# The inverse square root in a serial layer-norm recurrence: from ScalarE's table to VectorE arithmetic

## What is computed

```python
def step(carry, x):
    W1_s, b1_s = carry
    xq, xk, xv, eta_mb = x
    Z1 = xk @ W1_s + b1_s
    grad = _ln_fused_l2_bwd(Z1, xv - xk, ln_w, ln_b)
    Attn1 = jnp.tril(xq @ xk.swapaxes(-1, -2))
    b1_bar = b1_s - jnp.tril(eta_mb) @ grad
    Z1_bar = xq @ W1_s - eta_mb * Attn1 @ grad + b1_bar
    last_eta = eta_mb[:, :, -1, :, None]
    W1_new = W1_s - (last_eta * xk).swapaxes(-1, -2) @ grad
    b1_new = b1_s - jnp.sum(last_eta * grad, axis=-2, keepdims=True)
    out = xq + _ln(Z1_bar, ln_w, ln_b)
    return ((W1_new, b1_new), out)
```

## Time and profile before

| | us |
|---|---|
| Median of 3 runs (274.95 to 276.9) | 275.07 |
| The profiled execution | 269.17 |
| its span (first to last instruction) | 267.4 |
| busy in it: PE / DVE / ACT / POOL | 224.5 / 208.6 / 137.7 / 116.0 |
| mean granted clock of TensorE | 0.877 |

### The profile page before, as it was taken

How to read it: one execution, slowest core, us unless ns; L and a number is a source line. 1 busy time by engine, 2 the same in 40 slices (tenths; PEclk the granted TensorE clock), 3 DMA queues, 4 the chain that set the end, 5 groups by cost and what they waited for, 6 DMA issues and landing times.

```text
span 267.4 us, 5174 instructions
## 1 busy us (share of the span) xinstructions
PE 224.5 (84%) x1812; PEld 165.0 (62%) x1812; DVE 208.6 (78%) x548; ACT 137.7 (51%) x297; POOL 116.0 (43%) x151
## 2 busy tenths in 40 slices
PE   8389949799588997899399966996999889993993
PEld 6276425548356776577277654775778668782862
DVE  0873599998996999599949993959695996978551
ACT  1040363807374574558047607580477466867581
POOL 1840656309856454272237311725452263416044
PEclk9955999568879999799979957799799979998599
DMA  6945200012001200300020012000200034000012
GB/s 214 420 137 192 64 1 2 0 17 70 0 2 16 74 0 2 85 2 0 7 79 0 2 18 67 2 0 7 79 4 0 7 79 157 2 4 0 0 73 86
DMA packets 21544, 13.21 MB, mean 49 GB/s; under 512 B 10512, under 2 KB 19728, under 8 KB 21008
## 3 DMA queue, kind: packets, MB, share of 16 engines
q1 hardware_dynamic: 21088, 11.84, 15.0%
q10 hardware_dynamic: 432, 1.06, 1.1%
HBM read 11.02 MB, written 1.84 MB: 48 GB/s over the span
## 4 chain that ended last, share of the span: by engine, by line
PE 42%; DVE 31%; ACT 14%; issue 6%; DMA 3%; POOL 2%; DVEq 0%; POOLq 0%; SPq 0%; ACTq 0%
PE bank L964 11%; PE bank L983 6%; PE bank L900 6%; DVE pr L764 4%; DVE dW L769 4%; PE bank L935 4%; DMA x_bt<-in_x_bt 3%; DVE bank L716 3%; DVE pr L705 3%; ACT L473 2%; PE bank L997 2%; PE bank L908 2%; PE bank L917 2%; PE bank L973 2%; PE bank L1011 2%
## 5 line engine op out<-in xcount | busy, mean ns | idle before, releaser
L313 POOL TENSOR_TENSOR hh<-gate,upw 128x256 f32<-128x256 f32 x32 | 24.7, 772 | 56.8 <-ACT upw L460 56.8
L266 POOL TENSOR_TENSOR A<-A,mask 128x256 f32<-128x256 f32 x32 | 23.4, 733 | 38.4 <-ACT A L443 38.4
L935 PE MATMUL bank<-xqm,xkT 32*32 32x128 f32 x512 | 22.2, 291 | 20.5 <-DVE QP L654 11.5
L983 PE MATMUL bank<-down,hT 128*128 128x256 f32 x128 | 37.4, 422 | 0.0
L443 ACT ACTIVATE A<-bank,one 128x256 f32<-128x256 f32 x32 | 15.2, 474 | 39.5 <-PE bank L935 39.4
L964 PE MATMUL bank<-gup_hi,xnL_hi 128*128 128x512 f32 x64 | 32.1, 502 | 0.1
L935 PEld LDWEIGHTS bank<-xqm,xkT 32*32 32x32 f32 x512 | 12.7, 110 | 30.4 <-DVE QP L654 12.0
L964 PE MATMUL bank<-gup_hi,xnL_lo 128*128 128x512 f32 x64 | 28.5, 446 | 0.0
L964 PE MATMUL bank<-gup_lo,xnL_hi 128*128 128x512 f32 x64 | 28.2, 440 | 0.0
L983 PEld LDWEIGHTS bank<-down,hT 128*128 128x128 f32 x128 | 25.3, 219 | 2.5
L458 ACT ACTIVATE gate<-bank 128x256 f32<-128x256 f32 x32 | 12.3, 385 | 24.4 <-PE bank L964 24.2
(11 more groups left out here) (149 smaller groups left out, 491.1 us busy)
## 6 DMA issues: line engine op xcount, KB each, us to landing
wblk<-w_blocks SPq DMA_DIRECT2D x8, 512.0 KB, 4.1
x_bt<-in_x_bt SPq DMA_DIRECT2D x2, 512.0 KB, 6.7
sgpad<-in_gup SPq DMA_DIRECT2D x1, 1024.0 KB, 9.5
G<-in_gup SPq DMA_DIRECT2D x1, 1024.0 KB, 11.5
down<-in_down SPq DMA_DIRECT2D x1, 1024.0 KB, 6.3
xkT<-in_x_tok SPq DMA_DIRECT2D x1, 1024.0 KB, 4.8
out<-G SPq DMA_DIRECT2D x4, 256.0 KB, 2.5
wkv<-in_wkv ACTq DMA_DIRECT2D x1, 512.0 KB, 8.0
```

Of the source, the lines that this page charges most:

```text
L266: pool.tensor_tensor(scores, scores, mask_bc, ALU.mult).then_inc(S_["masked"], 1)
L313: pool.tensor_tensor(hh[:, i % 2, :, :], gate[:, i % 2, :, :], upw[:, i % 2, :, :], ALU.mult).then_inc(S_["h"], 1)
L935: ins = pe.matmul(bk[32 * b:32 * b + 32, P * hf:P * hf + P], xkT[32 * q:32 * q + 32, hf, j, GT * b:GT * b + GT], xqm[32 * q:32 * q + 32, j ...
L983: ins = pe.matmul(bank[7][:, 0:HS], hT[:, i % 2, r, :], down[:, 2 * e + r, :], start=(e == 0 and r == 0), stop=(e == 3 and r == 1))
```

## The change

In each minibatch the standard deviation from ACT and the reciprocal of two values go. DVE works out 1/sqrt(variance) itself. The bits of the variance are read as an integer, halved, negated and added to a constant, which gives a first value y0; a Newton step gives y1, a third-order step gives ri[0]; its square, ri[1], is the reciprocal of the variance. These are 12 instructions of 16 elements on a semaphore of their own, `root`, counting sxx and va. The triple sum S is split in three, of which two stand between the first steps. The products with S and with the rates read ri (SBUF) instead of rr (PSUM). fill(1) now stands ahead of the square of ri[0]. On ACT `step_std` and `preload_sqrt` go, with all their calls.

```diff
+ROOT_BITS, ROOT_A, ROOT_B, ROOT_OPS = float(0x5F1FFFF9), 0.703952253, 2.38924456, 12
...
-        sv = sb("sv", [P, 2, K])
+        va, y0, y1, ya, yb = (sb(name, [P, K]) for name in ("va", "y0", "y1", "ya", "yb"))
+        ri = sb("ri", [P, 2, K])
...
-            def step_std(n):
-
-                act.wait_ge(S_["vrc"], n + 1)
-                act.activation(sv[:, 0, :], sxx[:, :], ACT.Sqrt, bias=eps[:, 0:1], scale=1.0 / HD).then_inc(S_["rstd"], 1)
...
-            def preload_sqrt(n):
-
-                act.activation(warm[:, n:n + 1], eps[:, :], ACT.Sqrt)
...
             for j in range(1, NG):
-                if j > 2:
-                    step_std(2 * j)
...
-                if j > 1:
-                    preload_sqrt(2 * j)
-                    step_std(2 * j + 1)
                 for i in range(slot + FIRST_HALF[j], slot + SLOTS[j]):
                     expert_slot(i)
...
-                if 1 < j < NG - 1:
-                    preload_sqrt(2 * j + 1)
...
-                v.tensor_reduce(sxx[:, :], xx, AX.X, ALU.add).then_inc(S_["vrc"], 1)
+                v.tensor_reduce(sxx[:, :], xx, AX.X, ALU.add).then_inc(root, 1)
+                rooted = lambda k: v.wait_ge(root, n * ROOT_OPS + k)
                 done(7)
-                v.tensor_reduce(S[:, :, :], T[:, 2:5, :].rearrange("p k (t d) -> p k t d", d=HD), AX.X,
-                                ALU.add).then_inc(chain, 1)
-                v.wait_ge(S_["vrc"], n + 1)
-                v.tensor_scalar(sv[:, 1, :], sxx[:, :], 1.0 / HD, EPS, ALU.mult, ALU.add).then_inc(chain, 1)
+                v.tensor_reduce(S[:, 0, :], td(T[:, 2, :]), AX.X, ALU.add).then_inc(chain, 1)
+                rooted(1)
+                v.tensor_scalar(va[:, :], sxx[:, :], 1.0 / HD, EPS, ALU.mult, ALU.add).then_inc(root, 1)
+                v.tensor_reduce(S[:, 1, :], td(T[:, 3, :]), AX.X, ALU.add).then_inc(chain, 1)
+                rooted(2)
+                v.tensor_scalar(y0[:, :].bitcast(I32), va[:, :].bitcast(I32), -0.5, ROOT_BITS, ALU.mult, ALU.add).then_inc(root, 1)
+                v.tensor_reduce(S[:, 2, :], td(T[:, 4, :]), AX.X, ALU.add).then_inc(chain, 1)
+                rooted(3)
+                v.tensor_tensor(ya[:, :], y0[:, :], y0[:, :], ALU.mult).then_inc(root, 1)
+                rooted(4)
+                v.tensor_tensor(ya[:, :], ya[:, :], va[:, :], ALU.mult).then_inc(root, 1)
+                rooted(5)
+                v.scalar_tensor_tensor(out=y1[:, :], in0=ya[:, :], scalar=-ROOT_B, in1=y0[:, :],
+                                       op0=ALU.add, op1=ALU.mult).then_inc(root, 1)
+                rooted(6)
+                v.scalar_tensor_tensor(out=ya[:, :], in0=y1[:, :], scalar=ROOT_A * ROOT_A, in1=y1[:, :],
+                                       op0=ALU.mult, op1=ALU.mult).then_inc(root, 1)
+                rooted(7)
+                v.tensor_tensor(ya[:, :], ya[:, :], va[:, :], ALU.mult).then_inc(root, 1)
+                rooted(8)
+                v.tensor_scalar(yb[:, :], ya[:, :], -0.375 * ROOT_A, 1.25 * ROOT_A, ALU.mult, ALU.add).then_inc(root, 1)
+                rooted(9)
+                v.tensor_tensor(yb[:, :], yb[:, :], ya[:, :], ALU.mult).then_inc(root, 1)
+                rooted(10)
+                v.scalar_tensor_tensor(out=ri[:, 0, :], in0=yb[:, :], scalar=-1.875 * ROOT_A, in1=y1[:, :],
+                                       op0=ALU.add, op1=ALU.mult).then_inc(root, 1)
                 fill(1)
-
-                v.wait_ge(S_["rstd"], n + 1)
-                done(9)
-                v.reciprocal(rr, sv[:, :, :]).then_inc(chain, 1)
+                rooted(11)
+                v.tensor_tensor(ri[:, 1, :], ri[:, 0, :], ri[:, 0, :], ALU.mult).then_inc(root, 1)
+                rooted(12)
                 done(10)
-                v.tensor_tensor(rs[:, :, :], rr, S[:, 1:3, :], ALU.mult).then_inc(chain, 1)
-                v.tensor_tensor(rr, rr, sg_n.unsqueeze(1).broadcast_to([P, 2, K]), ALU.mult).then_inc(chain, 1)
+                v.tensor_tensor(rs[:, :, :], ri[:, :, :], S[:, 1:3, :], ALU.mult).then_inc(chain, 1)
+                v.tensor_tensor(rr, ri[:, :, :], sg_n.unsqueeze(1).broadcast_to([P, 2, K]), ALU.mult).then_inc(chain, 1)
```

More of the change, by code:

```diff
@@ L45 @@
 TOP = 0xFFFFF000
+I32 = mybir.dt.int32
+ROOT_BITS, ROOT_A, ROOT_B, ROOT_OPS = float(0x5F1FFFF9), 0.703952253, 2.38924456, 12
 BR = P + 1
@@ L152, in build @@
         pe_warm = sb("pe_warm", [P, 256])
-        warm = sb("warm", [P, 2 * NG])
         xqb = sb("xqb", [P, 2, B, HS])
@@ L187, in build @@
             pair0 pair0T rows rowsc xqb route gap s12 wx rdve
-            zero_w zero_d top hi split queries pair pair_done sc scored mask masked chain vrc rstd sg w wrow w_saved w_loaded b_saved
+            zero_w zero_d top hi split queries pair pair_done sc scored mask masked chain root sg w wrow w_saved w_loaded b_saved
             sgT sgp z0 z zc gu gact h hTp hT y g
@@ L514, in _ @@
             keys_out(1, (0, 1), 1, 4)
-            preload_sqrt(0)
-            step_std(0)
             queries_out(0)
@@ L522, in _ @@
             scores_out(0, 2)
-            step_std(1)
             scores_out(0, 3)
@@ L533, in _ @@
             queries_out(1)
-            step_std(2)
             high_half(2)
@@ L541, in _ @@
             act.activation(s12[:, 1, :], gap[:, :], ACT.Sigmoid, scale=-1.0).then_inc(S_["s12"], 1)
-            preload_sqrt(1)
             scores_out(1, 1)
-            step_std(3)
             slot = 0
             for j in range(1, NG):
-                if j > 2:
-                    step_std(2 * j)
                 if j == 5:
@@ L565, in _ @@
                 slot += SLOTS[j]
-                if j == 1:
-                    preload_sqrt(3)
-                    step_std(4)
                 if j + 1 < NG:
@@ L692, in minibatch @@
                 sg_td = sg.rearrange("p d t -> p t d")
-                chain = S_["chain"]
+                chain, root = S_["chain"], S_["root"]
                 done = lambda k: v.wait_ge(chain, n * OPS + k)
```

## The result

| us | before | after |
|---|---|---|
| Median (lowest to highest, 4 runs each, same chip) | 275.01 (272.03 to 276.9) | 289.86 (287.41 to 290.61) |
| the profiled execution | 269.17 | 287.41 |
| its span | 267.4 | 285.4 |
| mean granted clock of TensorE | 0.877 | 0.83 |

The change makes the kernel **slower, by 14.9 us in the medians**; the ratio of like executions is 1.0815, with a 95% interval of 1.0662 to 1.0969. The kernel before varies from 266.0 to 277.3 us over all its executions here and that of after by some 3 us, and the ratio and the two traces compare the fast executions of before with those of after (269.17 with 287.41, **18.2 us apart**), which is why they show more than the medians.

The account below looks back on a forecast made before the run. It took DVE alone to set the pace once its wait on ACT goes: 23.4 - 21.4 + 12.4 - 2 = +12.4 us on the profiled 269.17, making 281.6; between that and 287.5 it took 285, range 276 to 296.

Parts of the forecast that it names:

- waits on ACT removed: DVE's nine waits for ACT's square root disappear: 21.4 us saved.
- dependent steps: DVE's new chain: nine steps of 0.20 us, each waiting for the last, add 1.46 per minibatch, 23.4 in 16.
- turns with POOL: New DVE steps with both operands in SBUF alternate with POOL's instructions: 12.4 us added, bounds 0 and about 23.
- the end: After the scan, most of DVE's 2.56 us idle ahead of the second half's sums and ors goes: -2 us.
- DVE alone sets the pace: Once the wait on ACT is gone, whatever is added to DVE's chain is added to the kernel's time.
- Rival 4: PE becomes the pace at its lower clock: 1 to 3 us in a group or two, inside the range; no chance given.
- Rival 3: A step of DVE's chain costs 0.12 us, so the kernel gets faster, -7.6 us: 262 to 268; 6%.
- groups 2 to 6, first minibatch: one each: POOL's hh meets DVE's chain once in each of these five minibatches: 5 x 0.46 = 2.3 us.
- second minibatch: graze it, 1.0: In groups 2 to 6, later hh's of POOL fall beside DVE's chain or graze it: 1.0 us, between 0 and 2.3.
- The freed ACT at nothing: Roots, warm-ups and table loads removed from ACT were given no gain beyond the wait, as DVE sets the pace.
- rival 1: Turns with POOL cost nothing in DVE's chain; sum 0, so 275 us and no change; 13%.
- Rival 2: Each POOL instruction meeting DVE's chain costs its full length: +23 us, 292 to 298; 15%.

Follow-up runs that it names:

- e4: Against the kernel before: ACT's 16 roots and warm-ups left out, standard deviation set to the constant 1, nothing added; 257.54 us.
- e2_psum: Against the kernel after: same arithmetic, one operand of each new product in PSUM, one extra instruction writing ri[0] again; 276.83 us.
- e5_newton_psum: Against the kernel after: second Newton step for the third-order one, reciprocal for 1/variance, operands in PSUM, ux and fill(1) moved; 262.95 us.
- e7: Against the kernel after: ACT's roots, warm-ups and table loads put back, results unused; 287.8 us.
- e8_cast_psum: Against e2_psum: the cast of the routing indices (mif) writes to PSUM instead of SBUF; 273.17 us, ratio to before 1.0189.
- e6_one_step: Against the kernel after: third-order step left out, four dependent steps fewer, operands as in after; 271.69 us.
- e3_upper_late: Against the kernel after: upper_half(2) moved from fill(1) to fill(2) of minibatch (1,0), behind the rates; 286.9 us.

## Why the prediction was right or wrong

It gave the sign, the mechanism and a range that holds the time. It gave too small a loss: 285 for 289.86, and +12.4 against a profiled 269.17 where the profiles lie 18.2 apart (18.0 in the span). Term by term:

| Term, us | forecast | measured |
|---|---|---|
| waits on ACT removed | -21.4 | -21.3 (e4: -20.3) |
| dependent steps | +23.4 | +24.5 |
| turns with POOL | +12.4 | +18.8 |
| elsewhere in the scan | 0 | -0.9 |
| the end | -2 | -3.1 |
| sum | +12.4 | +18.0 |

*DVE alone sets the pace*: right. DVE has no wait on ACT left in the scan, and its share of the chain that ended last went from 31% to 72%. Rival 4 is out for this change. It is not for the removal alone: e4_no_root got 20.3 in the chain but 11.8 between the traces, with PE late at the end, so what hid PE after was the length of DVE's new chain.

*The steps*: right in kind, 1.1 short. The forecast let rs start at 2.71 behind the sum of squares; it starts at 2.80 (245.94 to 248.74 in (7,1)), because a step is 0.207 and not 0.20. y0 at 0.17 was the right end of its bounds. Rival 3 (0.12 a step) is out.

*The turns*: **this is the step that failed**, by 6.4: the term of 12.4 us measured 18.8, because the count of POOL's instructions that meet the chain came from the old trace. The rule held in the rows of after: DVE and POOL alternate, instruction by instruction (e2_psum to e5_newton_psum each have one place where DVE gets no turn; see the last section). The charges for single collisions were right as well: 1.84 and 1.79 in group 0 for 1.6 and 1.6. What was wrong is the count for the rest, "groups 2 to 6, first minibatch: one each" and "second minibatch: graze it, 1.0". I had charged 3.3 for those ten minibatches; they cost 8.0, by minibatch 2.70, 1.51, 0.60, 0.53, 0.41, 0.12, 0.60, 0.67, 0.45, 0.43. I had read when POOL works off the trace of before, although the change itself moves both sides: the chain is 1.5 us longer, and in before POOL's instructions had come behind ACT, which came behind its root. Group 2 has 4.2 of it. There before, ACT did the root at 88.67 and then a table load, and POOL's hidden product came at 91.63, after the product rs at 89.61; after, it comes at 102.92, while rs stands at 105.05, and the padding makes rs and the rates take 0.95 and 1.15. With the roots kept (e7) group 2 falls to 2.2, but groups 6 and 7 take what it gives: the total of the turns is stable, their places are not. So 2.0 of the 4.7 missed in these ten minibatches is shown to hang on ACT's order; that the rest comes of the longer chain is read from the timelines and not tested. Two smaller parts: in (1,0) I charged rs its 4.2 and forgot that the rates behind it (L739) also have ri and sig in SBUF, another turn of 0.6 (4.9 in all), though I had named ri x sig among the instructions with both operands in SBUF; group 7 took 2.3 for 1.7.

*The freed ACT at nothing*: right for the total, by e7 (0 to 2 us, and that a gain from putting the roots back), wrong as a statement on places, as above.

*The end*: right and a little more; both idle times are gone: zv follows 0.17 behind the instruction ahead of it (258.64 to 258.81), and ors has no idle time before it.

*From the profiled execution to the median*: the 5.9 us between the median of before and its profiled run were not a fixed addition. After's median is 2.5 above its own profiled run. The condition ("if it comes from PE inside the ring, DVE's pace will hide it") fits the runs on record. The times of before follow PE's granted clock: 266.0 us at 0.888, 268.7 to 269.6 at 0.876 and 0.877, 271.1 to 272.5 at 0.861 to 0.866, 272.9 to 274.9 at 0.853 and 0.854, 276.5 to 277.3 at 0.843 and 0.849 (one, of 276.4, at 0.855, is out of line). Those of after do not (287.4 at 0.830, 290.4 at 0.842), and the eleven of e8_cast_psum lie within 2.0 us from 0.832 to 0.870. That the clock is the cause no run shows by itself. The like comparison was 269 with 287, and by it the forecast of 281.6 was short by 5.8: 6.4 of turns and 1.1 of steps, less 2.0 at the end and elsewhere. The 3.4 us that the 285 has on top of 281.6 were a choice between two values and not worked out; that they come near the 2.5 of after is luck. They also hid the size of the loss: 12.4 of 269.17 is 4.6%, 285 beside 275.07 is 3.6%, and the ratio of like executions is 8.2%.

*Rivals*: rival 1 (turns cost nothing) falls with e2_psum, where taking them away gives 12.7 and with the cast 16.4. Rival 2 forecast whole durations; the time came near its lower end, but not by its rule: a step beside xqm of 0.46 loses 0.25 (they start 0.46 apart instead of 0.21), and the eight cost 1.8 and not 3.7. The Trainium skill, page "SBUF — State Buffer", section "Who interferes with whom", has the loser blocked for the whole instruction of the other; the rows agree where DVE arrives at its start (4.59 beside 4.58), and in a row of short ones (the xqm) DVE gets a turn between any two, so that it loses less than their whole durations.

*Signs named in advance*: no idle time ahead of rs, steps of 0.2 where POOL is idle and 0.42 to 0.65 where it is not, an rs of over 4 us in (1,0), ACT down to 97 us: all seen. PE's wait for QP rose to 19.4, just under the "over 20".

## What to carry to other kernels

Taking a round trip to another engine out of a chain pays only if the steps that replace it are shorter than the wait per turn: here nine steps of 0.21 and their turns cost 2.7 us a minibatch and took the place of a wait of 1.3, while six steps with PSUM operands beat it. In a chain of small DVE instructions, keep one operand or the result in PSUM wherever POOL works on SBUF; a step cost the same there (0.16 to 0.18 us), and it took some 16 us off here. When you price collisions, do not count them by the old trace alone, since the change shifts both sides: take POOL's busy share of the span times the new chain's clean length (an estimate worked out afterwards: 0.41 x 16 x 3.02 = 19.8 for the 18.8 of after, 0.43 x 16 x 2.19 = 15.1 for the 14.5 that e6_one_step has left; e3_upper_late, with the longest collision moved, lies below it, at 15.0), and look for single instructions elsewhere (the cast) that a faster chain will bring under a long POOL instruction.

## What was unexpected of the hardware

- A step of 16 elements, 0.17 us of work, can take 4.3: the cast of 16 values a partition waited for three POOL instructions, not for one (73.03 to 77.35; two of 1.97 and a mask end at 76.64 and 77.32). The same in e4_no_root (to 73.25, the mask to 73.22) and e5_newton_psum (3.86, to 76.17, the mask to 76.14). In the kernel before the same cast got its turn when the first of the two additions ended (69.64), and the products beside the xqm get one each time. When DVE gets in between two of POOL's instructions and when not, no run here shows.
- It is not the two inputs alone. The variance step (L709), one input and the output in SBUF, took 1.09 beside the padding (1.08 each); with its output in PSUM it took 0.17 to 0.18 throughout e2_psum. The reductions kept their 0.27 to 0.28 there (DVE in (7,0) of after, then POOL):

```profile
232.20 0.28 DVE L707 TENSOR_REDUCE S<-T 128x16 f32<-128x128 f32 x1
232.39 1.09 DVE L709 TENSOR_SCALAR va<-sxx 128x16 f32<-128x16 f32 x1
233.40 0.27 DVE L710 TENSOR_REDUCE S<-T 128x16 f32<-128x128 f32 x1
```

```profile
231.30 2.16 POOL L335 TENSOR_TENSOR sgpad<-sgT,small 128x512 f32<-128x512 f32 x2
```

- Steps with operands in PSUM take 0.16 to 0.18 and start 0.20 to 0.22 apart, no slower than in SBUF at this size.
